# Limiting the indirect DMAs in flight to two of each kind in a sorted mixture-of-experts layer

## Reference

```
scores = sigmoid(xf @ gate_w + bias);  top_scores, top_idx = top_k(scores, 2)
w[t, e] = top_scores, normalised, 0 elsewhere
hact = gelu(xf @ up_w[e] + up_b[e]);  eo = hact @ down_w[e] + down_b[e]      # 8 experts, 128 -> 512 -> 128
shared = (gelu(xf @ sw_up + sb_up) @ sw_down + sb_down) * 0.1
out = shared + sum_e 0.1 * w[t, e] * eo
x = x + 0.5 * out / (max|out| + 1e-6)
```

## Time and profile before

| | |
|---|---|
| device time, median of 3 runs | 1561.59 us (1555.86 to 1562.26) |
| the profiled execution | 1572.32 us, of which the span of instructions is 1570.2 us |
| PE busy | 1286.0 us (82%) |
| DVE busy | 964.0 us (61%) |
| ACT busy | 827.2 us (53%) |
| POOL busy | 676.2 us (43%) |
| indirect DMAs | 128 scatters, 156 puts |

### The profile page before, as it was taken

One profiled execution on the slowest core, in us unless ns is written; L12 is line 12 of the kernel. 1 busy time (PEld: TensorE's weight loads), 2 busy tenths in 40 slices (PEclk: granted clock), 3 DMA queues, 4 the chain that ended last, 5 costly groups with the idle time before them and its releaser, 6 DMA issues. The chain is left out here.

```text
span 1570.2 us, 30207 instructions
## 1 busy us (share of the span) xinstructions
PE 1286.0 (82%) x8434; PEld 725.2 (46%) x8434; DVE 964.0 (61%) x2082; ACT 827.2 (53%) x1988; POOL 676.2 (43%) x880
## 2 busy tenths in 40 slices
PE   2987999999999698884789974988998796568993
PEld 1761222222222376553689861221222254568983
DVE  5787898898898186500223744899989740023455
ACT  0221788888888434421356653666665451235661
POOL 3123223223220222474445531788788537354442
PEclk9995999999999799786899996899998888689996
DMA  5970222212220100212457742444444121346774
GB/s 116 170 155 1 72 73 82 71 43 69 71 72 22 19 16 2 59 49 83 126 159 209 223 120 77 150 155 140 150 141 147 64 71 60 97 127 177 221 212 129
DMA packets 161935, 164.76 MB, mean 105 GB/s; under 512 B 31389, under 2 KB 113771, under 8 KB 161800
## 3 DMA queue, kind: packets, MB, share of 16 engines
q1 hardware_dynamic: 150592, 145.92, 34.2%
q0 software_dynamic: 9088, 16.94, 3.1%
q10 hardware_dynamic: 2120, 0.28, 0.1%
HBM read 115.45 MB, written 45.90 MB: 103 GB/s over the span
## 5 line engine op out<-in xcount | busy, mean ns | idle before, releaser
L1193 DVE TENSOR_REDUCE at_nm<-at_mx 128x2 f32<-128x1024 f32 x256 | 303.9, 1220 | 40.5 <-PE at_mx L1036 39.2
L1139 ACT ACTIVATE at_probs<-at_ring 128x512 f32<-128x512 f32 x512 | 269.4, 605 | 47.4 <-PE at_ring L1048 45.8
L1539 ACT ACTIVATE m_hidden<-m_pU,mw_up_b 128x128 f32<-128x128 f32 x624 | 178.7, 371 | 127.7 <-PE m_pU L1745 70.6
L1489 POOL DMA_INDIRECT pair_rows<-m_y,m_y_id x156 | 152.5, 977 | 203.0 <-DVE m_y L1686 123.3
L1754 PE MATMUL m_pD<-m_down_all,m_hidden 128*128 x1248 | 175.9, 286 | 37.5 <-ACT m_hidden L1539 30.9
L2236 POOL TENSOR_TENSOR ss_hc<-ss_h,ss_c_all 128x512 f32<-128x512 f32 x128 | 161.7, 1270 | 52.3 <-DVE ss_h L2406 45.5
L1745 PE MATMUL m_pU<-m_hidden,m_up_now 128*128 128x128 f32 x1248 | 174.4, 285 | 7.3 <-issue 6.5
L1754 PEld LDWEIGHTS m_pD<-m_down_all,m_hidden 128*128 128x128 f32 x1248 | 158.9, 199 | 43.7 <-issue 42.9
L1048 PE MATMUL at_ring<-at_qq,at_kk 51*128 51x512 bf16 x512 | 163.3, 386 | 7.1 <-ACT at_probs L1139 6.1
L1036 PE MATMUL at_mx<-at_kk,at_qq 48*128 48x512 bf16 x512 | 156.0, 399 | 13.1 <-DVE at_nm L1193 8.0
L1745 PEld LDWEIGHTS m_pU<-m_hidden,m_up_now 128*128 128x128 f32 x1248 | 160.6, 201 | 9.6 <-issue 9.6
(11 more groups left out here) (319 smaller groups left out, 1948.7 us busy)
## 6 DMA issues: line engine op xcount, KB each, us to landing
m_up_now<-in_L_ffn_up_w_dram SPq DMA_DIRECT2D x156, 256.0 KB
ss_dtb<-ss_dt_rows SPq DMA_DIRECT2D x128, 256.0 KB
sorted_rows<-empty_row SPq DMA_DIRECT2D x2, 5070.0 KB, 47.2
m_xb<-sorted_rows SPq DMA_DIRECT2D x156, 65.0 KB
m_hidden<-pair_rows SPq DMA_DIRECT2D x32, 256.0 KB
at_qq<-q_stack SPq DMA_DIRECT2D x64, 96.0 KB, 2.2
at_kk<-k_stack SPq DMA_DIRECT2D x64, 96.0 KB, 2.3
m_down_all<-in_L_ffn_down_w_dram SPq DMA_DIRECT2D x16, 256.0 KB, 4.3
```

The lines of the kernel that those rows point to most:

```text
L1139: act.activation(probs[:, (slot % 2) * GH + ORDER[j], :], ring[bank][:, :], ACT.Exp, scale=SCALE).then_inc(s.exp_done, 1)
L1193: dve.tensor_reduce(nm[group % 2][:, 2 * (pair % 2) + parity, 2 * half:2 * half + 2], mx[parity][:, :, :], AX.X, ALU.max, negate=True).the ...
L1489: pool.indirect_dma_start(pair_rows, bass.IndirectOffsetOnAxis(ap=y_id[j % Y_BUFS][:, :], axis=0), y[j % Y_BUFS][:, :], None, bounds_check ...
L1539: act.activation(hid[j % T_BUFS][:, k, :], pU[j % 2][:, k * P:(k + 1) * P], ACT.Gelu, bias=v.up_b[:, bass.ds(e, 1), k:k + 1].rearrange("p ...
```

## The change

Every scatter waits until the scatter two places in front of it has landed, and every put until the put two places in front has landed. The four semaphores of the lists become two, used in turn over all 64 scatters. The waits at the ends of lists are written in terms of these two and mean the same as before.

```
+SCATTERS, PUTS = 2, 2
...
-    scattered = [[sem(f"{tag}_scattered{h}{k}") for k in range(2)] for h in range(HALVES)]
+    scattered = [sem(f"{tag}_scattered{i}") for i in range(SCATTERS)]
...
             for half in range(HALVES):
-                for k in range(2):
-                    sp.wait_ge(scattered[half][k], 16 * HT)
+                for i in range(SCATTERS):
+                    sp.wait_ge(scattered[i], 16 * (2 * HT * (half + 1) // SCATTERS))
...
+            def wait_scattered(n):
+
+                for i in range(SCATTERS):
+                    pool.wait_ge(scattered[i], 16 * (n // SCATTERS))
+
             def scatter(half, k, t):
-                at_tile = half * HT + t
+                at_tile, n = half * HT + t, (2 * half + k) * HT + t
+                if n >= SCATTERS:
+                    pool.wait_ge(scattered[n % SCATTERS], 16 * (n // SCATTERS))
                 pool.indirect_dma_start(sorted_rows, ...
-                                        ).then_inc(scattered[half][k], 16)
+                                        ).then_inc(scattered[n % SCATTERS], 16)
 
             def put(j):
                 pool.wait_ge(s.y_ready, j + 1)
+                if j >= PUTS:
+                    pool.wait_ge(y_out[(j - PUTS) % Y_BUFS], 16 * ((j - PUTS) // Y_BUFS + 1))
                 pool.indirect_dma_start(pair_rows, ...
...
-            pool.wait_ge(scattered[0][0], 16 * HT)
+            wait_scattered(HT)
...
-            pool.wait_ge(scattered[1][0], 16 * HT)
+            wait_scattered(3 * HT)
```

## The result

The change makes the kernel slower. The median is 1584.79 us (1581.9 to 1587.47, 4 runs) against 1558.72 us for the kernel before beside it (1554.47 to 1562.26, 4 runs). The ratio is 1.0167, with a 95% interval from 1.0138 to 1.0196, 26 us. The prediction had 1538 as the likeliest time. The profiled executions are only 15.2 us apart (1587.47 and 1572.32), because that of before lies 13.6 us above the 1558.72 and that of after 2.7 us above its own median. So the two traces account for 15 of the 26.

The account below looks back on a forecast made before the run. POOL's unbroken scatters were taken to use up something every engine needs, starving PE. The front's 15 us less 3 for the puts made 12 a layer, 24 in all: 1561.6 - 24 = 1538 us, range 1523 to 1588.

Parts of the forecast that it names:

- The price of a wait: In the lists: two scatters per landing plus 0.76 us, 1.5 us a scatter (1.42 to 1.70), so 0.23 more each.
- The relief of the front: Layer's front: at 1.5 us a scatter PE has no or short holes; block 0 starts near 718 instead of 743.
- the balance: In the lists: the scatter pace at which PE at full pace no longer starves, 1.53 us, estimated from one pause.
- The first rival: Lists: the crawl comes from POOL's work, not its pace, and lasts as long; 1588 us, chance 0.30 including the recording case.
- The step that failed: Interleaved scatters and puts: waits free, seventeenth put 22 us earlier; less 7.6 for PE, 15 us a layer won (0 to 22).
- lives on its lead: Interleaved part: PE starves again but draws on blocks done ahead, losing 4 blocks of 1.9 us, 7.6 us.
- third rival: Interleave and puts: the same DMAs must pass, so the front's gain is given back; within 8 us of 1562, chance 0.12.
- if holes in the interleave grow by what the front gained: Interleaved scatters and puts: a sign, named beforehand, that the forecast is wrong; no size given.
- List (1, 0): Second half's first list: priced at 1.5 us a scatter, 22.5 us, last scatter at 735.4, first put about 740.
- Puts alone: Puts after the interleaved part: 1.42 to 1.99 us each with waits; 3 us a layer lost (0 to 10).
- The sum: Whole kernel: 15 us won less 3 lost, 12 a layer, 24 in all, giving 1538 us.
- The recording: Rival: writing profile records holds the crawling engines, so timed runs lack the crawl; 1588 at most, counted within the 0.30.

Follow-up runs that it names:

- the paced kernel: Kernel before plus two small POOL operations (0.43 us) behind each scatter of the three lists, no waits; on chip B 1558.08 us against 1569.34, ratio 0.9933.
- four in front: Kernel as changed, but each wait is for the DMA four places ahead instead of two; on chip B 1572.95 us against 1569.56 before, ratio 1.0003.
- the front waits: Kernel before with waits only in lists (0, 0) and (0, 1); 1556.6 us on chip B, ratio 0.9928 to before; 1.0127 to 1.0141 on A, C, D.

## Why the prediction was wrong

**The price of a wait** was 1.5 us a scatter with 1.70 as upper end. It measured 1.66 and 1.63 in list (0, 0), where the same fifteen intervals took 1.33 and 1.34 before, so a wait cost 0.32 and 0.28 us and not 0.23. The mechanism was as described: the chain of waits after the change shows 0.02 + 0.03 + 0.71 = 0.76 us from a landing to the next start, as taken, and landings above 2.07.

**The relief of the front** was right. No holes in the shared expert at a pace of 1.66, where the balance was put at 1.53, and block 0 turned 58 us after the first scatter, where 56 was predicted and 81 measured before. That a slower pace is enough for this relief was argued in the prediction and is shown by the paced kernel on B. Whether the pace or the number in flight counts stays open. The first rival, waits without relief, is refuted. That its time came nearest, 1588, is luck.

**The step that failed** and carried the forecast is the seventeenth put "at 780, where it is at 802 now", and with it the 15 us that remained after a deduction of 7.6. The prediction said PE "lives on its lead" in the interleaved part. It does not. With its 31 DMAs in an unbroken row, PE comes nearly to a stop (53 matmuls in 40 us), and DVE and ACT too. The kernel as changed on B has 51 there. Before the change that same part ran with pauses, because POOL was often waiting for results, and PE got 205 matmuls through, 203 with four in front and 172 with the front waits. The lead is used up, to the last block but one. This is the prediction's third rival, relief given back, and the sign it named ("if holes in the interleave grow by what the front gained"). The front waits on B show its size by itself: 6 to 7 us a layer are left in place of 15, and that with a first put 7 us earlier than before. With the change as a whole, 2.0 and 3.4 are left.

**List (1, 0)** was priced like the quiet ones, "its last scatter at 710.9 + 2.0 + 22.5". It took 35.1 us, not 22.5. In order of time this step fails before the other. The first put came 96 us after the first scatter in place of 78, about 5 us of that from the two quiet lists and 12.6 from this one, and POOL's 31 DMAs from there end at 135, so at most 8 to 9 us a layer could be won even had PE kept its lead. Either failure alone leaves 6 to 9 us, both together 2.0 and 3.4. The prediction moved block 0 forward by 20 us, and did not ask what block 0's loads, which now start with this list, do to the landings it waits for. A part of the chain of waits in the second layer's list (1, 0):

```profile
1352.61 4.29 DMA sorted_rows<-mw_rows,m_index
1356.90 0.02 issue
1356.92 0.03 POOLq L1491
1356.95 0.71 issue
1357.67 4.08 DMA sorted_rows<-mw_rows,m_index
...
1364.43 5.44 DMA sorted_rows<-mw_rows,m_index
```

Landings of 4 and 5 us, where 128 rows of the last put landed in 2.07. On B, the waits in the two later lists make the first put 14.8 us later in the first layer, and cost 3.6 us at the seventeenth: PE's crawl hides most of the list's delay. Without crawl all of it is paid.

**Puts alone** were given 3 us a layer (bounds 0 and 10), from a pace of at most 1.99. They measured 2.17 and 2.23, over the 2.1 that the prediction named as a sign of being wrong, and 7.2 and 13.2 us lost; on B 9.7 and 10.1. The mistake is that of the list: the term was sized by a quiet landing and one loaded row. The rule of the Trainium skill that was weighed there ("DMA: Bandwidth & Descriptors", latency and other measured facts: HBM's access 2 us at high load in place of 0.2) came nearer for the pace: it made an estimate of 2.3 us a put. Its 15 us a layer are too many. The seven landings in that chain from 1344 to 1378, of which three stand above, take 3.1 to 5.4 us, 3.95 on average, which fits an addition of that order (2.07 + 1.8); no run tells where in a landing the time is spent.

**The sum** then is -2.0 and +7.2 in the first layer, -3.4 and +13.2 in the second, where each was to be -15 and +3. **The recording** as cause of the crawl stays open. The two kinds of chip run the same program 110 us apart in the timed executions as well, so the crawl is not confined to the profiled one. But every execution here, timed ones too, has its span and clock on record, so none shows the kernel without any recording. What makes the engines crawl, and why on some chips only, was not found.

## What to carry to other kernels

When a wait for a landing is priced, take the landing under the load that will be there once the change has moved the work, not the one of a quiet stretch. Here 2.1 became 3 to 5 us. Two in front bound in all three lists and at 38 of the 156 puts, and four in front hardly at all. A lead that one engine gains is worth only what the next stretch leaves of it, so look at the stretch behind, and ask what keeps it as fast as it is: here, as far as these traces tell, it was the pauses of POOL, which had to wait for late results. And before tuning against an effect that no releaser explains, run the unchanged kernel on more than one chip: the best version on chip B, the front waits, wins 0.7% there and loses 1.3% on the other three.

## What was not expected of the hardware

One and the same program takes 1457 to 1459 us on three chips and 1569 us on a fourth. On the latter the work of PE, ACT, DVE and SP's queue slows down while POOL issues indirect DMAs 1.27 us apart, after some 14 of them. At 1.66 or 1.75 us apart there is no slowing, at least over the 32 scatters of two lists. On the first three, the traces show nothing of it at 1.27.

An indirect DMA of 128 rows whose landing is seen 2.07 us after its start in a quiet stretch lands after 3.1 to 5.4 us with a DMA share of 0.73. Two small operations of GpSimd, 0.43 us together, between two such DMAs lengthen the interval from 1.27 to 1.75 us, while one of 0.15 us is free.
